# Six steps of attention issued ahead of the branch on the mask, split and reordered input loads, and a later load of expert 1's weights

## The chip, the cores and the metric

One NeuronCore of one Trainium2 chip runs the whole program. The metric is the device time of one execution in microseconds (us), median of several runs. All times below are from one profiled execution unless the text says otherwise; its clock starts at the span's start.

## The reference, cut to what matters

`x` is 2048 x 256, the context 1601 x 256, all float32. The layer is a gated cross attention followed by a gated mixture of experts:

```python
x = x + tanh(g_xattn) * xattn(layernorm(x), ctx, mask)   # 16 heads of 64, Wq, Wk, Wv, Wo
x = x + tanh(g_ffn)   * moe(layernorm(x))                # 8 experts, top 2, hidden 512

scores = einsum('bthd,bThd->bhtT', q, k) / sqrt(64)
scores = where(mask, scores, finfo(float32).min)
attn   = softmax(scores);  out = einsum('bhtT,bThd->bthd', attn, v) @ Wo
# moe: out += (silu(x @ W1[e].T) * (x @ W2[e].T)) @ W3[e].T * w_e  for the two chosen experts
```

The mask of this case lets every query see only the last 401 of the 1601 keys (or fewer). The kernel reads the whole mask, finds out whether that is so, and branches: a fast attention over the last 401 keys, or a general one over all keys. In every run here the fast one is taken.

## The kernel before, in words

The five engines run their own instruction streams and meet at semaphores: PE (TensorE) does the matmuls, ACT (ScalarE) exponentials and most copies out of PSUM, DVE (VectorE) masking, maxima and the block transposes, POOL (GpSimd) the scaling by 1/sum and the scatters, SP (SyncE) only issues DMAs, in program order, all on one queue.

**The opening.** SP issues the loads: the last 401 columns of the context and Wk (both count on `kv_in`), x in four groups of 512 rows (`x_in[g]`), Wq, the mask in four parts of 800 KB (`mask_in[c]`), Wv, Wo, Wg. PE waits for `kv_in`, computes the keys of all eight head pairs (`kT`, L1143), transposes the first 512 normalised rows (`transpose_xn`, L1160) and computes the queries of chunk 0 (L1149). DVE normalises x group 0, takes the statistics of groups 1 to 3, and reduces the last columns of each mask part (L813). ACT copies keys and queries out of PSUM and sums the other mask words (`mask_words`, L605), four passes. POOL turns each mask part into a bias (L462). Then DVE reduces the flag, PE sums it over partitions with a one-column matmul, DVE compares it, and every engine waits for `flag_ready`, reads `plainflag` and branches (`last_block_only`). `settled` makes each engine wait for the rest of the opening, in the fast branch of DVE and POOL too.

**The fast attention** is a hand-written software pipeline of 140 steps (`STEPS_FAST`). A chunk is one head pair for 512 queries (32 chunks); it has four "duos" d (128 queries, two heads), one per step. In step n:

- PE: scores of duo n (`scores`, L1216); in steps 0 to 7 one eighth of V (`values`, L1227), in steps 8 to 10 the late transposes of x; the queries of the next chunk when n % 4 is 1; from step 11 on probabilities times V of an older chunk in two halves (`probs_v`, L1241), from step 18 on half an output projection every fourth step (L1251).
- DVE: in steps 0 to 5 two rows of tiles normalised; the reciprocal of duo n-1's sums, mask and row minimum of duo n (L984), block transposes of duo n-2 (L996).
- ACT: the exponentials of duo n (L636), copies of V, of queries and of attention outputs.
- POOL: scaling of duo n-1 (L525).
- SP and ACT: 16 "regroup" DMAs for each chunk (L316) that move the transposed blocks from `blocksT` across partitions into `probsT`. SP issues 12 of them and ACT 4 (8 each for the last chunk). `probs_v` of a chunk waits for all 16.

Scores of duo d wait until DVE has masked duo d-2 (four PSUM banks); each eighth of V waits until ACT has copied the one before (`v_ready`), since they share one bank.

**The end of attention.** SP loads expert 0's three weight matrices (1.5 MB) in chunk 29, the regroups of chunks 30 and 31, then expert 1's 1.5 MB, then waits for the last regroups, for the schedule of tiles (`sched_ready`) and for the scatters of the regrouped rows (`scattered`), and loads the first tiles of rows (`load_tile`, L353). The expert stage runs 128-row tiles, expert after expert, each with 8 + 8 matmuls and two transposes on PE; routing of the last 512 rows is interleaved with its first tiles. Every tile's result is added to the output by an indirect DMA from POOL.

Of the kernel before, what the change touches and what calls it, by code (L numbers as in the profile page):

```python
# [13 lines left out]
P = 128  # L14
# [51 lines left out]
SCHED_STEP = 133  # L66
LAST_WO = DUOS + 10
# [8 lines left out]
def build(nc, x, ctxT, mask, g_xattn, g_ffn, Wq, Wk, Wv, Wo, WgT, W1T, W2T, W3T, out):  # L76
    with ExitStack() as ctx:
# [64 lines left out]
        with ExitStack() as attn:  # L142
# [3 lines left out]
            with ExitStack() as fast:  # L146
# [4 lines left out]
                with ExitStack() as early:  # L151
                    wk_sb = sb("wk_sb", [P, KT, H * HD], F32, early)
                    mask8 = sb("mask8", [P, NT, SKP], U8, early)
                    xn = sb("xn", [P, GT, D], F32, early)
# [9 lines left out]
                inv_sum = sb("inv_sum", [P, RING_P], F32, fast)  # L164

# [34 lines left out]
        x_in, w_in, g_in = [sem(f"x{g}_in") for g in range(NR)], sem("w_in"), sem("g_in")  # L200
        wo_in = sem("wo_in")
        kv_in, wv_in = sem("kv_in"), sem("wv_in")
# [81 lines left out]
        def settled(eng):  # L284

            eng.wait_ge(w_in, 16)
            eng.wait_ge(wo_in, 16)
            eng.wait_ge(q_ready, 1)
            eng.wait_ge(k_ready, HP)
            eng.wait_ge(wv_in, 16)  # L290
            eng.wait_ge(xnT_ready, 2)
            eng.wait_ge(biases_ready, MASK_DMAS)
            eng.wait_ge(words_seen, MASK_DMAS)
            eng.wait_ge(mask_seen, MASK_DMAS)

# [29 lines left out]
        def _(sp):  # L325
            sp.dma_start(ctx_last[:, :, 0:LASTK], ctxT[:, LAST0:].rearrange("(k p) n -> p k n", p=P)).then_inc(kv_in, 16)
            sp.dma_start(wk_sb[:, :, :], Wk.rearrange("(k p) n -> p k n", p=P)).then_inc(kv_in, 16)
            for g in range(NR):
                sp.dma_start(xs[:, GT * g:GT * g + GT, :], x[g * GQ:(g + 1) * GQ, :].rearrange("(t p) d -> p t d", p=P))\
                  .then_inc(x_in[g], 16)  # L330
            sp.dma_start(wq_sb[:, :, :], Wq.rearrange("(k p) n -> p k n", p=P)).then_inc(w_in, 16)
            sp.wait_ge(mask_pad, 1)
            for c in range(MASK_DMAS):
# [21 lines left out]
            with sp.If(last_block_only(sp)):  # L355
# [81 lines left out]
        def _(pool):  # L437
            pool.memset(mask8[:, :, SKP - 4:], 0).then_inc(mask_pad, 1)
            pool.dma_start(gates[:, 0:1], g_xattn.partition_broadcast(P)).then_inc(g_in, 16)
            pool.dma_start(gates[:, 1:2], g_ffn.partition_broadcast(P)).then_inc(g_in, 16)  # L440
# [19 lines left out]
            for c in range(MASK_DMAS):  # L460
# [55 lines left out]

            def fast_attention():
                settled(pool)

                def scale(d):  # L520

                    pool.wait_ge(inv_ready, d + 1)
                    u = 2 * d % RING_P
                    duo = probs[:, u:u + 2, 0:LASTK]
                    pool.tensor_tensor(duo, duo, inv_sum[:, u:u + 2].unsqueeze(2).to_broadcast([P, 2, LASTK]), ALU.mult)\  # L525
                        .then_inc(scaled, 1)

                for n in range(STEPS_FAST):
                    if n == 2:
                        pool.memset(probsT[:, :, NS - 1, :, :, :], 0.0).then_inc(pads_set, 1)  # L530
                    if 1 <= n <= DUOS:
                        scale(n - 1)
                    r, s = group_of(n)
# [965 lines left out]
```

## Time and profile before

| | us |
|---|---|
| median of 3 runs | 665.11 |
| lowest and highest run | 661.04, 665.76 |
| the profiled execution's own time | 661.78 |
| its span, first to last instruction | 660.0 |
| mean granted clock of PE | 0.986 of full speed |
| PE busy | 622.1 (94%) |
| DVE, ACT, POOL busy | 393.6, 287.7, 309.2 |

The profiled execution has 1.8 us outside its span. A line of a group gives the code line, engine, operation and tiles, then the count, busy time and mean duration in ns, then the idle time before it and who ended it. Matmul durations in a timeline overlap, since matmuls are pipelined, so the distance between two starts is the better price.

### The profile page before, as it was taken

The page shows a single profiled execution, that of the slowest core. Times are in us where ns is not written, and L with a number is a line of the kernel's source. Part 1 is how long each engine was busy: PE and PEld are TensorE (multiplying, and loading weights), DVE is VectorE, ACT ScalarE, POOL GpSimd, SP SyncE. Part 2 cuts the span into 40 slices and gives each one's busy share as a digit, 9 for nine tenths or more (in the row PEclk, how much of TensorE's full clock was granted, in tenths as well). Part 3 has the DMA queues.
Part 4 walks back from the last instruction along what each step waited for, and adds up shares of the span by engine and source line. Part 5 has one row for each costly group of instructions (what it writes and reads, how often), then busy time and mean ns, then how long its engine had stood idle before and what let it go on. Part 6 is the DMA issues. An engine that isn't in the chain of part 4 may idle for free.

```text
span 660.0 us, 10752 instructions
## 1 busy us (share of the span) xinstructions
PE 622.1 (94%) x2958; PEld 346.2 (52%) x2959; DVE 393.6 (60%) x1187; ACT 287.7 (44%) x744; POOL 309.2 (47%) x272
## 2 busy tenths in 40 slices
PE   4599999999999999999999999699999999999994
PEld 2244445454555544455554555256666666666663
DVE  3767788888987878988769977333251212221211
ACT  1556665656555564564545554023322222222221
POOL 2345565555564587564685564502464222222221
PEclk9989999999999999999999998899999999999998
DMA  8904577676766776757677569969556322333221
GB/s 273 333 1 104 144 168 170 142 167 146 163 149 150 161 186 163 166 130 184 134 193 179 135 158 249 269 186 377 161 142 131 49 41 42 47 48 48 46 23 22
DMA packets 92652, 95.37 MB, mean 144 GB/s; under 512 B 11056, under 2 KB 86704, under 8 KB 92592
## 3 DMA queue, kind: packets, MB, share of 16 engines
q1 hardware_dynamic: 69968, 71.64, 41.9%
q10 hardware_dynamic: 15840, 14.07, 9.4%
q0 software_dynamic: 6784, 8.95, 8.2%
q8 instruction: 27, 0.44, 0.3%
q14 instruction: 33, 0.27, 0.1%
HBM read 27.72 MB, written 12.36 MB: 61 GB/s over the span
## 4 chain that ended last, share of the span: by engine, by line
PE 77%; POOL 6%; DMA 5%; issue 4%; DVE 4%; ACT 2%; ACTq 1%; POOLq 0%; SPq 0%; DVEq 0%
PE ps_s L1396 17%; PE ps_s L1216 14%; PE ps_o L1241 13%; PE ps_o L1424 8%; PE ps_a L1149 7%; PE ps_a L1251 7%; POOL probs L525 3%; POOL x_regrouped L513 2%; DMA out_dram<-yg,ids 2%; PE ps_o L1227 2%; PE ps_t L1417 2%; PE ps_s L1143 2%; DVE blocksT L996 2%; DMA probsT<-blocksT 1%; DMA wk_sb<-Wk_dram 1%
## 5 line engine op out<-in xcount | busy, mean ns | idle before, releaser
L525 POOL TENSOR_TENSOR probs<-probs,inv_sum 128x802 f32<-128x802 f32 x128 | 194.8, 1524 | 154.5 <-DVE inv_sum L975 153.7
L636 ACT ACTIVATE probs<-probs,neg_max 128x401 f32<-128x401 f32 x256 | 159.3, 624 | 147.1 <-DVE neg_max L984 147.0
L984 DVE CUSTOM_DVE_ANT_0 probs<-ps_s,biases 128x401 f32<-128x401 f32 x256 | 136.9, 573 | 52.5 <-PE ps_s L1216 51.6
L1396 PE MATMUL ps_s<-w_sb,xgT 128*128 x296 | 139.5, 594 | 1.4 <-ACT xgT L732 1.4
L996 DVE STREAM_TRANSPOSE blocksT<-probs 128x832 f32<-128x832 f32 x128 | 133.2, 1040 | 9.0 <-POOL probs L525 9.0
L564 POOL DMA_INDIRECT out_dram<-yg,ids x36 | 56.0, 1555 | 159.4 <-DVE yg L1108 136.5
L1241 PE MATMUL ps_o<-probsT,v_sb 128*64 128x512 f32 x512 | 125.0, 612 | 4.4 <-DMA probsT<-blocksT 4.4
L1216 PEld LDWEIGHTS ps_s<-kT,qT 64*128 64x128 f32 x1024 | 82.9, 187 | 78.6 <-DVE neg_max L984 42.2
L1216 PE MATMUL ps_s<-kT,qT 64*128 64x201 f32 (+1 forms) x1024 | 122.0, 357 | 1.4 <-issue 1.4
L1096 DVE TENSOR_TENSOR gated<-ps_s,silu 128x512 f32<-128x512 f32 x37 | 25.6, 692 | 117.5 <-PE ps_s L1396 112.1
L1396 PEld LDWEIGHTS ps_s<-w_sb,xgT 128*128 128x128 f32 x296 | 53.0, 191 | 39.5 <-issue 37.9
L745 ACT COPY gatedT<-ps_t 128x512 f32<-128x512 f32 x36 | 21.1, 585 | 120.4 <-PE ps_t L1417 120.4
L1424 PE MATMUL ps_o<-w_sb,gatedT 128*128 x288 | 68.1, 380 | 0.0
L1251 PE MATMUL ps_a<-wo_sb,oT 128*128 128x256 f32 x240 | 61.5, 400 | 3.3 <-ACT qT L593 3.0
L1149 PE MATMUL ps_a<-xnT,wq_sb 128*128 128x512 f32 x128 | 63.2, 616 | 0.8 <-ACT xnT L597 0.8
L1241 PEld LDWEIGHTS ps_o<-probsT,v_sb 128*64 128x64 f32 x512 | 31.7, 137 | 58.9 <-issue 53.4
L1424 PEld LDWEIGHTS ps_o<-w_sb,gatedT 128*128 128x128 f32 x288 | 52.0, 191 | 5.5
L1251 PEld LDWEIGHTS ps_a<-wo_sb,oT 128*128 128x128 f32 x240 | 44.2, 194 | 16.2 <-ACT qT L593 9.6
L636 ACT ACTIVATION_READ_ACCUMULATOR probs<-probs,neg_max 128x1 f32 x256 | 47.8, 187 | 0.0
L1108 DVE TENSOR_SCALAR yg<-ps_o,xg 128x256 f32<-128x256 f32 x36 | 17.4, 484 | 41.3 <-PE ps_o L1424 41.3
L513 POOL DMA_INDIRECT x_regrouped<-rows,place x32 | 31.5, 984 | 9.1 <-issue 8.3
L1149 PEld LDWEIGHTS ps_a<-xnT,wq_sb 128*128 128x128 f32 x128 | 21.9, 189 | 23.9 <-issue 23.9
(142 smaller groups left out, 420.9 us busy)
## 6 DMA issues: line engine op xcount, KB each, us to landing
probsT<-blocksT SPq DMA_DIRECT2D x285, 96.0 KB
probsT<-blocksT SPq DMA_DIRECT2D x95, 128.0 KB
probsT<-blocksT ACTq DMA_DIRECT2D x99, 96.0 KB
xg<-x_regrouped SPq DMA_DIRECT2D x39, 129.0 KB, 2.1
probsT<-blocksT ACTq DMA_DIRECT2D x33, 128.0 KB
w_sb<-W1T_dram SPq DMA_DIRECT2D x8, 512.0 KB, 9.5
w_sb<-W2T_dram SPq DMA_DIRECT2D x8, 512.0 KB, 10.2
w_sb<-W3T_dram SPq DMA_DIRECT2D x8, 512.0 KB, 10.5
```

The costliest lines, as they stand in the source:

```text
L513: pool.indirect_dma_start(out=x_regrouped, out_offset=bass.IndirectOffsetOnAxis(ap=place[:, c, t:t + 1], axis=0), in_=rows[:, c, t, :], in ...
L525: pool.tensor_tensor(duo, duo, inv_sum[:, u:u + 2].unsqueeze(2).to_broadcast([P, 2, LASTK]), ALU.mult)\
L564: pool.indirect_dma_start(out=out, out_offset=bass.IndirectOffsetOnAxis(ap=ids[:, k % RING:k % RING + 1], axis=0), in_=yg[:, k % 2, :], in ...
L636: act.activation(probs[:, b, 0:LASTK], probs[:, b, 0:LASTK], ACT.Exp, bias=neg_max[:, b:b + 1], scale=-1.0, accum_out=sum_exp[:, b:b + 1]) ...
L984: dve.tensor_tensor_reduce(probs[:, b, 0:LASTK], ps_s[u % 4][:, 0:LASTK], biases[:, tile, :], HD ** -0.5, 3e38, ALU.add, ALU.min, neg_max[ ...
L996: dve.transpose(blocksT[:, c % 2, :, :, t * 32:(t + 1) * 32].rearrange("p c u n -> p u c n"), probs[:, u:u + 2, :].rearrange("p u (c n) -> ...
L1149: mm = pe.matmul(ps_a[:, :], wq_sb[:, k, p * P:(p + 1) * P], xnT[:, k, i * GQ:(i + 1) * GQ], start=(k == 0), stop=(k == KT - 1))
L1216: mm = pe.matmul(ps_s[(2 * d + odd) % 4][:, k0:k1], qT[h0:h0 + HD, c % 2, t * P:(t + 1) * P], kT[h0:h0 + HD, c % HP, k0:k1], start=True, s ...
L1241: mm = pe.matmul(ps_o[odd * HD:(odd + 1) * HD, :], v_sb[:, s, 2 * (c % HP) + odd, :], probsT[:, c % 2, s, :, odd, :], start=(s == 0), stop ...
L1251: mm = pe.matmul(wo_bank(g, half)[:, n * D:(n + 1) * D], oT[:, c % 4, t * P:(t + 1) * P], wo_sb[:, c % HP, :], start=(c == 2 * g), stop=(c ...
L1396: mm = pe.matmul(bank[:, :], xgT[:, buf, k, :], w_sb[:, bass.ds(expert, 1), (n * KT + k) * FH:(n * KT + k + 1) * FH].squeeze(1), start=(k ...
L1424: mm = pe.matmul(ps_o[:, 0:D], gatedT[:, k, :], w_sb[:, bass.ds(expert, 1), 2 * KT * FH + k * D:2 * KT * FH + (k + 1) * D].squeeze(1), sta ...
```

## The change

1. **Loads (SP).** The order becomes: x group 0, context, first half of Wk (`kv_in`), first half of Wq (`w_in[0]`), mask part 0, Wv, mask parts 1 to 3, second half of Wk (`wk1_in`), x groups 1 to 3, second half of Wq (`w_in[1]`), the two gates (two tiny DMAs that POOL issued before), Wo, Wg.
2. **Six steps (`PRE = 6`) ahead of the branch.** Steps 0 to 5 of all engines are issued before the flag is read. PE makes keys of pairs 0 and 1 only, then the transposes and queries of chunk 0, then the steps; the other keys come in steps 0, 6, 7, 8, 10 and 12. V moves two steps later (steps 2 to 9), the late transposes of x to steps 20 to 22. The flag's matmul is in step 5. ACT's mask pass c + 1, DVE's and POOL's parts of the mask are in steps 0 to 2 or 3; the tanh of the gates is in step 6.
3. **LayerNorm of x groups 1 to 3 (DVE).** Statistics in steps 6 to 9, three tiles each, the reciprocal square root in step 10, normalising in steps 11 to 16.
4. **`settled`** is waited for only in the general branch. Two tiles get memory of their own (`wk_sb`, `xn`), and the mask pass writes its unused result to `blocksT` instead of `probs`.
5. **Expert 1.** SP issues `load_expert(1)` after the wait for the last regroups instead of before it.

The diff, cut:

```diff
+PRE = 6
+K_STEPS = {0: 2, 6: 3, 7: 4, 8: 5, 10: 6, 12: 7}
+XN_STEP = 20
...
+            load_x(0)
+            sp.dma_start(ctx_last[:, :, 0:LASTK], ...).then_inc(kv_in, 16)
+            load_half(wk_sb, Wk, 0, kv_in)
+            load_half(wq_sb, Wq, 0, w_in[0])
+            sp.wait_ge(mask_pad, 1)
+            load_mask(0)
             sp.dma_start(wv_sb[:, :, :], Wv.rearrange("(k p) n -> p k n", p=P)).then_inc(wv_in, 16)
+            for c in range(1, MASK_DMAS):
+                load_mask(c)
+            load_half(wk_sb, Wk, 1, wk1_in)
+            for g in range(1, NR):
+                load_x(g)
+            load_half(wq_sb, Wq, 1, w_in[1])
...
-                load_expert(sp, 1)
                 expert_there(0)
                 for slot in range(2):
                     sp.wait_ge(probsT_in[slot], 16 * REGROUP * CHUNKS // 2)
+                load_expert(sp, 1)
                 sp.wait_ge(sched_ready, 2)
                 sp.wait_ge(scattered, 16 * 2 * GT * (NR - 1))
...
 # ACT
+            def step_of(n):
+                if n == PRE:
+                    gates_tanh()
+                if 3 <= n < 3 + 2 * NS:
+                    values(n - 3)
+                if n - 1 in K_STEPS:
+                    keys(K_STEPS[n - 1])
...
+                if n < DUOS:
+                    exps(n)
+                if n + 1 < MASK_DMAS:
+                    mask_words(n + 1)
...
+            keys(0)
+            keys(1)
+            move_xnT(0)
+            move_xnT(1)
+            queries(0)
+            mask_words(0)
+            for n in range(PRE):
+                step_of(n)
...
 # DVE
+            def step_of(n):
+                if n == PRE - 1:
+                    flag_everywhere()
+                if PRE <= n < PRE + 4:
+                    statistics(GT + 3 * (n - PRE), GT + 3 * (n - PRE) + 3)
+                if n == PRE + 4:
+                    mean_and_rsqrt(GT, NT, 11)
+                if PRE + 5 <= n < PRE + 11:
+                    for t in (2 * (n - PRE - 5), 2 * (n - PRE - 5) + 1):
+                        normalise(GT + t)
...
+                if n == PRE - 3:
+                    mask_flag()
...
 # PE
+            def step_of(n):
+                if n == PRE - 1:
+                    pe.wait_ge(flag_step, 5)
+                    pe.matmul(ps_t[1][0:1, 0:1], ones[:, 0:1], rowflag[:, 0:1], start=True, stop=True).then_inc(flag_sum, 1)
+                r, s = group_of(n)
+                if n < DUOS:
+                    scores(n)
+                if 2 <= n < 2 + 2 * NS:
+                    values(n - 2)
+                if n in K_STEPS:
+                    if K_STEPS[n] == 4:
+                        pe.wait_ge(wk1_in, 16)
+                    keys(K_STEPS[n])
...
+            keys(0)
+            keys(1)
+            transpose_xn(0)
+            transpose_xn(1)
+            pe.wait_ge(w_in[0], 16)
+            pe.wait_ge(xnT_ready, 2)
+            queries(0)
+            for n in range(PRE):
+                step_of(n)
```

POOL's `step_of(n)` does `mask_biases(n)` for n below 4 and `scale(n - 1)`; its memset of `probsT` moves from step 2 to step 5, behind waits for the three users of the mask tile, whose memory `probsT` shares.

## Rows read from the trace of the kernel before

**Rows 1.** The page: busy time of an engine, and its costliest groups

```profile
PE 622.1 (94%) x2958; PEld 346.2 (52%) x2959; DVE 393.6 (60%) x1187; ACT 287.7 (44%) x744; POOL 309.2 (47%) x272
...
L984 DVE CUSTOM_DVE_ANT_0 probs<-ps_s,biases 128x401 f32<-128x401 f32 x256 | 136.9, 573 | 52.5 <-PE ps_s L1216 51.6
...
L996 DVE STREAM_TRANSPOSE blocksT<-probs 128x832 f32<-128x832 f32 x128 | 133.2, 1040 | 9.0 <-POOL probs L525 9.0
```

**Rows 2.** Busy time of the engines by stretch, with granted clock

```profile
22.40:33.04 10.64, 3.02 (x14) 1.43 (x13) 6.07 (x16) 7.08 (x12) 4.81 (x5) 0.87 0.87 306
33.04:38.00 4.96, 4.96 (x14) 2.62 (x16) 2.64 (x9) 1.44 (x5) 0.93 (x1) 0.60 0.00 0
...
55.14:100.61 45.47, 44.16 (x249) 22.61 (x248) 36.71 (x102) 30.58 (x84) 24.58 (x17) 1.00 0.68 156
```

**Rows 3.** Timeline of the opening: start, length, engine, line, operation

```profile
9.69 12.71 PE L1143 MATMUL ps_s<-ctx_last,wk_sb 128*128 128x401 f32 x32 [9.69 <-DMA wk_sb<-Wk_dram]
...
14.36 0.51 ACT L590 ACTIVATE kT<-ps_s 128x401 f32<-128x401 f32 x1 [1.11 <-PE ps_s L1143]
...
15.70 0.51 ACT L590 ACTIVATE kT<-ps_s 128x401 f32<-128x401 f32 x1 [0.84 <-PE ps_s L1143]
16.20 4.01 DVE L794 BATCH_NORM_STATS2 halves<-xs 128x6 f32<-128x256 f32 x12
...
22.23 1.04 PE L1160 MATMUL ps_t<-ident,xn 128*128 128x128 f32 x8
...
26.08 0.58 ACT L593 COPY qT<-ps_a 128x512 f32<-128x512 f32 x1 [0.94 <-PE ps_a L1149]
...
26.56 1.21 ACT L605 ACTIVATE probs<-mask 128x1200 f32<-128x1200 int32 x1
26.62 1.53 POOL L462 TENSOR_SCALAR biases<-mask 128x1604 bf16<-128x1604 uint8 x1 [0.66 <-DMA mask<-mask_dram]
...
27.95 1.21 ACT L605 ACTIVATE probs<-mask 128x1200 f32<-128x1200 int32 x1
...
33.04 1.71 PE L1216 MATMUL ps_s<-kT,qT 64*128 64x201 f32 x8 [1.38 <-issue]
...
35.37 0.63 ACT L636 ACTIVATE probs<-probs,neg_max 128x401 f32<-128x401 f32 x1 [4.72 <-DVE neg_max L984]
```

**Rows 4.** Timeline of PE alone, steps 4, 5, 6 and 23

```profile
48.72 1.99 PE L1227 MATMUL ps_o<-wv_sb,ctx_last 128*128 128x512 f32 x4
50.63 0.95 PE L1216 MATMUL ps_s<-kT,qT 64*128 64x201 f32 x8
...
55.14 0.95 PE L1216 MATMUL ps_s<-kT,qT 64*128 64x201 f32 x8
...
100.61 0.95 PE L1216 MATMUL ps_s<-kT,qT 64*128 64x201 f32 x8
```

**Rows 5.** The chain that ended last, end of attention

```profile
414.96 9.22 DMA probsT<-blocksT
...
424.22 3.68 PE ps_o L1241 x16
...
432.35 0.40 PE ps_t L1391 x2
```

**Rows 6.** Busy time by stretch, one microsecond of attention's end

```profile
416.00:417.00 1.00, 1.00 (x4) 0.24 (x2) 0.00 (x0) 0.00 (x0) 0.69 (x2) 0.50 1.16 200
```

**Rows 7.** DMA packets, 415.3 to 420.4 and 420.4 to 422.4

```profile
DMA packets 1186, 1.08 MB, mean 211 GB/s; under 512 B 168, under 2 KB 1175, under 8 KB 1186
...
DMA packets 398, 0.64 MB, mean 318 GB/s; under 512 B 66, under 2 KB 254, under 8 KB 398
```

**Rows 8.** Timeline of SP's queue at attention's end

```profile
415.27 0.67 SPq L274 DMA_DIRECT2D w_sb<-W1T_dram  x1
...
416.52 0.57 SPq L274 DMA_DIRECT2D w_sb<-W3T_dram  x1
429.97 8.77 SPq L353 DMA_DIRECT2D xg<-x_regrouped  x8
```

More of the change, by code:

```diff
@@ L198, in build @@
         ps_a = psum("ps_a")
-        x_in, w_in, g_in = [sem(f"x{g}_in") for g in range(NR)], sem("w_in"), sem("g_in")
+        x_in, w_in, g_in = [sem(f"x{g}_in") for g in range(NR)], [sem("w0_in"), sem("w1_in")], sem("g_in")
         wo_in = sem("wo_in")
-        kv_in, wv_in = sem("kv_in"), sem("wv_in")
+        kv_in, wk1_in, wv_in = sem("kv_in"), sem("wk1_in"), sem("wv_in")
         mask_in = [sem(f"mask{c}_in") for c in range(MASK_DMAS)]
@@ L458, in _, with mask_biases @@
                       allow_small_or_imprecise_dtypes=True).then_inc(const_ready, 1)
[L460 removed]
+            def mask_biases(c):
                 pool.wait_ge(mask_in[c], 16)
@@ new lines, in exps, with values @@
+            def exps(d):
+                for u in (2 * d, 2 * d + 1):
+                    b = u % RING_P
+                    act.wait_ge(masked_ready, u + 1)
+                    act.activation(probs[:, b, 0:LASTK], probs[:, b, 0:LASTK], ACT.Exp, bias=neg_max[:, b:b + 1],
+                                   scale=-1.0, accum_out=sum_exp[:, b:b + 1]).then_inc(probs_ready, 1)
+            def values(c):
+                s, half = c // 2, c % 2
+                w = TAIL if s == NS - 1 else P
+                act.wait_ge(pads_ready, 2)
+                act.wait_ge(v_ps, c + 1)
+                act.copy(v_sb[0:w, s, 8 * half:8 * half + 8, :],
+                         ps_o[0:w, :].rearrange("p (h d) -> p h d", h=8)).then_inc(v_ready, 1)
@@ L1036, in _ @@
+            for n in range(PRE):
+                step_of(n)
+            def fast_attention():
+                for n in range(PRE, STEPS_FAST):
+                    step_of(n)
             with dve.If(last_block_only(dve)):
@@ new lines, in scores @@
+            def scores(d):
+                c, t = d // GT, d % GT
+                if t == 0:
+                    pe.wait_ge(q_ready, c + 1)
+                    if c < HP:
+                        pe.wait_ge(k_ready, max(2, c + 1))
+                if d >= 2:
+                    pe.wait_ge(masked_ready, 2 * d - 2)
+                for k0, k1 in ((0, 201), (201, LASTK)):
+                    for odd in range(2):
+                        h0 = odd * HD
+                        mm = pe.matmul(ps_s[(2 * d + odd) % 4][:, k0:k1], qT[h0:h0 + HD, c % 2, t * P:(t + 1) * P],
+                                       kT[h0:h0 + HD, c % HP, k0:k1], start=True, stop=True)
+                        if k0:
+                            mm.then_inc(scores_ready, 1)
@@ new lines, in values @@
+            def values(c):
+                s, half = c // 2, c % 2
+                w = TAIL if s == NS - 1 else P
+                if c == 0:
+                    pe.wait_ge(wv_in, 16)
+                else:
+                    pe.wait_ge(v_ready, c)
+                for k in range(KT):
+                    mm = pe.matmul(ps_o[0:w, :], ctx_last[:, k, s * P:s * P + w],
+                                   wv_sb[:, k, half * 512:(half + 1) * 512], start=(k == 0), stop=(k == KT - 1))
+                mm.then_inc(v_ps, 1)
@@ new lines, in out_projection, with halves_before @@
+            def out_projection(g, half):
+                pe.wait_ge(oT_ready, 2 * g + 2)
+                for n in range(2):
+                    t = 2 * half + n
+                    for c in (2 * g, 2 * g + 1):
+                        mm = pe.matmul(wo_bank(g, half)[:, n * D:(n + 1) * D], oT[:, c % 4, t * P:(t + 1) * P], wo_sb[:, c % HP, :],
+                                       start=(c == 2 * g), stop=(c == 2 * g + 1))
+                mm.then_inc(wo_ps, 1)
+            def halves_before(n):
+                return max(0, min(CHUNKS, (n - 15) // 4))
```

468 lines of the change are left out of this document (213 added, 255 removed).

## The prediction, made before the changed kernel was run

> **What bounds the kernel now.** I read the page first: PE is busy for 94% of the span and no other engine for more than 60% [rows 1]. So the end moves when PE stands still for less, or works at a higher clock, and an edit to DVE or SP counts only where PE waits for it. Next the busy time by stretch, to find where PE does stand still. From the end of the first queries to the first scores it works 3.0 of 10.6 us, and in the 5 us behind that it is busy at a mean granted clock of 0.60. From step 6 to step 23 (55.14 to 100.61) it works 44.16 of 45.47 us [rows 2], so there is nothing to win there, and whatever is won before step 6 stays won. Third, the opening's timeline: scores of step 0 start at 33.04, with everything that they need except the flag there since the query copy at 26.66; the last 1.38 us are the branch ("issue") [rows 3]. Last, the chain at the end of attention: 9.22 us pass from the last regroup's issue to its landing at 424.2, then 8.1 us of PE work for the last chunk, and then the transpose of the first expert tile at 432.35 [rows 5].
>
> **Part 1: when does step 6 start?** I follow the new program with the old durations.
>
> Kv_in: the same 1.46 MB is ahead of it as before (x group 0 and half of Wk in place of the second half), and keys started at 9.69 [rows 3]. But it is now about 1,024 pieces in place of 512 (x rows are 1 KB, half rows of Wk 2 KB, whole ones 4 KB). The trace doesn't price that at the start. From below it is 0, since bytes are equal; from above 2.2 us, 512 pieces more at the 1,186 packets in 5.1 us of the regroups [rows 7]. I take 0.7, nearer the lower end, since the opening's loads read long rows from DRAM. Keys: 10.4.
>
> Two keys, not eight: before, the second was in PSUM at 14.36, that is 4.7 us after the start, cold clock included [rows 3]. So 15.1. Transposes to copied queries took from 22.23 to 26.66, 4.4 us, paced by PE and ACT in turn [rows 3]; xn is ready in time: it was by 16.2 before, when DVE went on to the other groups [rows 3], and x group 0 now lands first. Scores of step 0: 19.5, and not 33.0.
>
> From there ACT is what is late. One mask pass costs 1.4 us (26.56 to 27.95), two exponentials 2 x 0.63 = 1.3, a key copy 0.5, a query or V copy 0.6 [rows 3]. ACT's order is: mask pass 0, exps 0, pass 1, key copy, exps 1, pass 2, query copy, exps 2, pass 3, first V copy. That is 4 x 1.4 + 3 x 1.3 + 0.5 + 0.6 + 0.6 + 0.2 of waiting = 11.4, so V's first eighth is copied at 30.9. The masks are there: before, POOL got the last part at 26.6 [rows 3] after 7.9 MB; now 6.3 MB go ahead of it, so it lands at about 22, and pass 3 starts at 29. PE meanwhile has done steps 1 and 2 and step 3's scores, and stands for about 2 us. From 30.9 it is the bound: three eighths of V at 1.91 (48.72 to 50.63), two scores at 0.9 and one set of queries at 1.9 [rows 4] make 9.4, so step 5 ends at 40.3. The branch costs up to 1.38 [rows 3], or nothing if PE still has matmuls queued while it is taken; the flag is compared some 5 us ahead of it. I take 0.7. **Step 6 starts at 41.0, before at 55.14** [rows 4].
>
> But less has been done by then. Five of the eight keys are still to come, at 1.34 each (14.36 to 15.70) [rows 3] 6.7 us, and two eighths of V more than before, 3.8 us. The stretch to step 23 took 45.47 and becomes 45.47 + 6.7 + 3.8 = 56.0; I take off 0.2 of its 1.31 idle [rows 2], since queued keys cover some of it: 55.8. The late transposes only move inside it. Step 23: 41.0 + 55.8 = 96.8, before 100.61. **Part 1 gains 3.8 us.** The bulk of the 14 us was work postponed, not removed: what really goes is the idle time at 26 to 33 and the half-clock stretch behind it, and 2 us of new idle time, 0.7 of branch and 0.7 of loads come in.
>
> Its ends: with kv_in on time, a covered branch and no idle time in the stretch, 0.7 + 0.7 + 0.9 more, 6.1. With kv_in at the upper end and the branch in full, 2.2 less; with DVE's burst (below) on top, 0 to 0.5.
>
> POOL: it does four mask biases at 1.53 [rows 3] and the scalings beside each other, some 3 us a step in steps 1 to 3, where ACT's steps last 3.3. The bigger memset in step 5 stands in front of scaling 4, wanted by DVE only in step 6. Nothing. SP: the two gate DMAs are now in its queue behind the loads; nobody reads them before step 6. SP's own branch comes at about 37 and its first regroups with it; they are wanted in step 11, some 20 us later. Nothing. PE's wait for `wk1_in` in step 7 is for bytes landed by 25. Nothing.
>
> The LayerNorm of groups 1 to 3 lay in the opening for free. Now it sits in DVE's steps 6 to 16. Statistics cost 4.01 / 12 = 0.33 each [rows 3], 1.0 a step for four steps; step 10 has some 23 small operations, about 3.3 us (estimate: between the statistics' end at 20.2 and the next engine-bound work there was room for no more than 6); then 0.7 a step. A DVE step is 2 x 0.5 + 1.0 + 0.2 = about 2.2 [rows 1]. Over the eleven steps: 24 + 4 + 3.3 + 4.2 = 35.5. PE has 0.9 x 11 scores, four eighths of V, five keys, two queries, four halves of probabilities times V at 1.87: 35.6. A tie, with DVE starting earlier and two steps of slack through the banks. I book 0, with 2 us against.
>
> **Part 2: expert 1 later.** The packets decide it. Between 415.3 and 420.4 all but 11 of 1,186 packets are under 2 KB, so they are regroups, though expert 1's loads are issued from 415.27 on: they lie behind SP's regroups in the same queue [rows 7, 8]. Only between 420.4 and 422.4 are larger ones there, 144 of 398, and many of these belong to POOL's scatter [rows 7]. So expert 1 meets only the last microsecond of ACT's regroups. I take 0.4 us; ends 0 and 2.2, the time that PE stands before 424.22 if a landing is delayed wholly by it.
> The Trainium skill (DMA: Bandwidth & Descriptors, "Queues, rings and completion order") says that each DMA engine takes turns between the queues by packets and keeps order in one. By the first half the edit should free half of the bandwidth for ACT's regroups; by the second it frees nothing until SP's own are through, and the trace agrees with that half.
> The other side: expert 1's 1.5 MB now stand in SP's queue ahead of the row tiles (L353), which were issued from 429.97 [rows 8], just in time for 432.35 [rows 5]. Issued at 424, 1.5 MB take 4.9 us at 318 GB/s and 7.4 at the regroups' 211 [rows 7], and the row tile itself 2.4 from issue to transpose; so that starts at 431.3 or at 433.8. It costs nothing up to about 432, 1.5 at the worst. Expert 1 itself is wanted some tiles later.
>
> **The sum.** 3.8 + 0.4 = 4.2 us less than the profiled 661.78 gives 657.6. That execution stands 3.3 below the median of the three runs, 665.11, which themselves spread over 4.7. Against the median: **660.9**.
>
> **The rivals.**
>
> *A. More than this: the waits go without replacement.* Step 6 at 39.6, and the last regroups land up to 2 us earlier, so that PE's hole before 424.22 closes: 6.1 + 2 = 8 us, 657. For it: PE does stand there for 2.2 us. Against it: the packet sizes [rows 7].
>
> *B. DVE's LayerNorm burst or a cold clock takes most of it.* In step 10 DVE is away for 3.3 us while PE has only 2.2 us of work. And PE idles 2 us in step 3; in attention's end, after two such gaps, it was granted 0.50 for several microseconds [rows 6]. One such spell costs half its length, about 2 us, DVE's jam 0 to 2. Left: 0 to 2 us, 664.
> The Trainium skill (TensorE: Matmul & The Clock Gate, "HAM oscillation") warns that gaps between bursts bring PE back to 1.2 GHz, again and again; it speaks against a kernel that starts attention early but in pieces.
>
> *C. Slower.* The whole head stays at 1.2 GHz. Steps 0 to 5 hold 18 us of PE work (six scores 5.3, four eighths 7.6, a key, two queries) strung between ACT's mask passes. If their gaps keep the granted clock at one half, as in 33 to 38 [rows 2], 18 us more are needed, of which 2 are the idle time: 665.11 + 16 - 4 = 677. It decides from the point where more than 8 us of PE work are done at half clock. Against it: from 19.5 to 28 PE has work nearly without a gap.
>
> *D. No change.* The first row tile behind expert 1 costs 1.5 [rows 5, 8] and kv_in 2.2: what is left is 1 us, 664.
>
> **How the numbers follow.** Forecast 0.50 (its own range 658 to 663), A 0.20, B 0.20, C 0.04, D 0.06. The range needs A's better half, B and D, and the 4.7 by which runs of the same kernel differ: 654.5 to 665.0. The kernel can tell about 1% from no change, 6.6 us. Faster by more needs A, or the forecast's upper end with a favourable median: 0.22. Slower by over 1% is C and a rest: 0.04. Between: 0.74.
>
> **What would show it.** Right: scores of step 0 at 19 to 20, a hole of 1.5 to 2.5 us in PE in step 3 ended by ACT's first V copy, step 6 at 40 to 42, step 23 near 97, the last regroup landing no more than 0.5 us earlier against the first scores of step 127. Wrong: PE waiting for DVE in steps 10 to 13, granted clock under 1 between 13 and 45, kv_in after 11.5, or PE waiting for a row tile at the end of attention. Most of all I may be wrong in ACT's order of copies and passes, since every microsecond there is one of the total.

## The result: 656.6 us, and the profile after

The changed kernel takes 656.64 us (median of 4 runs, 655.02 to 657.84), the kernel before 665.01 on the same chip (661.04 to 665.76). The ratio is 0.988 with a 95% interval of 0.984 to 0.991: faster by 8.4 us, 1.2%. The forecast was 660.9, so the direction was right and the gain half of what came. The profiled execution after took 657.01 us, that of before 661.78; these two are only 4.7 apart, and why that pair shows less than the medians is the first thing to find out. Medians and ratios here and below leave out two executions that stand far apart from all others: one of the kernel before beside experiments 1 to 4 (1264.92 us) and one of experiment 3 (906.37 us).

**Where it went, by marks.** In each trace I note the start of the scores of steps 0, 6, 23 and 127 and of the first expert tile's transposes. This splits the span into a head, a stretch that nothing in the change should touch (23 to 127), attention's end, and the experts.

| start at (us) | step 0 | step 6 | step 23 | step 127 | first tile | span |
|---|---|---|---|---|---|---|
| before | 33.04 | 55.14 | 100.61 | 401.72 | 432.35 | 660.0 |
| after | 18.56 | 38.38 | 94.30 | 395.22 | 427.60 | 655.3 |

The head gains 6.3 at step 23 and 6.5 at step 127; from there to the first tile the new kernel takes 32.4 and the old one 30.6, so 1.7 is given back; from the tile to the end both take 227.7.

The page after, engine PE:

```profile
PE 622.2 (95%) x2958; PEld 344.4 (53%) x2959; DVE 389.9 (59%) x1187; ACT 286.9 (44%) x744; POOL 308.2 (47%) x270
```

PE is as busy as before, 622.2 against 622.1 [rows 1]: no work was removed, only idle time. The windows of the head (columns: stretch, length, then busy time and instructions of PE, weight loads, DVE, ACT, POOL; granted clock, DMA share, GB/s):

```profile
18.56:38.38 19.82, 18.31 (x79) 8.77 (x79) 14.16 (x46) 15.59 (x39) 12.68 (x9) 1.00 0.61 200
38.38:94.30 55.92, 55.02 (x278) 27.48 (x277) 45.76 (x147) 33.59 (x90) 25.94 (x18) 1.00 0.58 133
```

In steps 0 to 5 PE works 18.31 of 19.82 us; before, in the 10.6 us ahead of step 0 alone, it worked 3.0 [rows 2]. Its clock is at the full 2.4 GHz, where before it stood at a mean of 0.60 behind that gap [rows 2]. The timeline of the opening, engines PE and ACT:

```profile
8.57 5.67 PE L1220 MATMUL ps_s<-ctx_last,wk_sb 128*128 128x401 f32 x8 [8.57 <-DMA wk_sb<-Wk_dram]
...
14.27 0.51 ACT L632 ACTIVATE kT<-ps_s 128x401 f32<-128x401 f32 x1 [2.15 <-PE ps_s L1220]
...
18.40 1.21 ACT L648 ACTIVATE blocksT<-mask 128x1200 f32<-128x1200 int32 x1
...
18.56 0.95 PE L1284 MATMUL ps_s<-kT,qT 64*128 64x201 f32 x8 [0.68 <-ACT qT L636]
...
21.52 1.20 ACT L648 ACTIVATE blocksT<-mask 128x1200 f32<-128x1200 int32 x1
...
24.32 1.20 ACT L648 ACTIVATE blocksT<-mask 128x1200 f32<-128x1200 int32 x1
...
25.52 0.57 ACT L636 COPY qT<-ps_a 128x512 f32<-128x512 f32 x1
...
27.22 1.20 ACT L648 ACTIVATE blocksT<-mask 128x1200 f32<-128x1200 int32 x1
...
28.41 0.57 ACT L680 COPY v_sb<-ps_o 128x512 f32<-128x512 f32 x1
...
29.03 1.98 PE L1297 MATMUL ps_o<-wv_sb,ctx_last 128*128 128x512 f32 x4 [1.51 <-ACT v_sb L680]
...
36.56 1.88 PE L1227 MATMUL ps_a<-xnT,wq_sb 128*128 128x512 f32 x4
```
```profile
38.38 0.95 PE L1284 MATMUL ps_s<-kT,qT 64*128 64x201 f32 x8
...
94.30 0.95 PE L1284 MATMUL ps_s<-kT,qT 64*128 64x201 f32 x8
```

Read it against the steps of the prediction: keys at 8.57, second key copied from 14.27, scores of step 0 at 18.56, ACT's four mask passes (18.40, 21.52, 24.32, 27.22) between the copies, V's first copy at 28.41, and PE standing 1.51 us for it. That is the only hole of the six steps. Step 6 starts at 38.38 with no bracket behind it: it comes straight behind the queries of 36.56, so the branch is hidden.

The chain at attention's end, and SP's queue there:

```profile
408.48 9.27 DMA probsT<-blocksT
...
417.79 3.68 PE ps_o L1311 x16
...
425.92 1.69 issue
427.60 0.42 PE ps_t L1486 x2
```
```profile
417.82 0.38 SPq L277 DMA_DIRECT2D w_sb<-W1T_dram  x1
...
418.87 0.47 SPq L277 DMA_DIRECT2D w_sb<-W3T_dram  x1
421.14 8.75 SPq L384 DMA_DIRECT2D xg<-x_regrouped  x8
```

The last regroup takes 9.27 us to land (before 9.22 [rows 5]), though expert 1 is now issued only behind it, at 417.82. So part 2 seems to have won nothing. And PE now stands 1.69 us before the first tile, whose rows are issued at 421.14, behind expert 1's three matrices. That looks like what rival D priced at 1.5, but it isn't a wait for the rows. The time from issue to landing of the eight row tiles (`xg`):

```profile
DMA to landing us min/median/max: 2.2/3.5/4.5
```

Even the slowest of them takes 4.5 us, so the first has landed by 425.6, before the last output projection ends at 425.9. The chain books the 1.69 us as "issue": PE waits for nothing that the profile shows. What part 2 is worth is settled by runs, not by one pair.

### The profile page after: what moved, and what is told of

Same layout as the page of the kernel before. It is cut to its first block, busy times and chain, and to the rows that moved or that the text cites. A ratio compares the mean times of both kernels' runs of the same rounds, so it can differ in the third digit from the quotient of the medians.

```text
span 655.3 us, 10748 instructions
## 1 busy us (share of the span) xinstructions
PE 622.2 (95%) x2958; PEld 344.4 (53%) x2959; DVE 389.9 (59%) x1187; ACT 286.9 (44%) x744; POOL 308.2 (47%) x270
## 4 chain that ended last, share of the span: by engine, by line
PE 76%; POOL 6%; DMA 5%; DVE 5%; issue 4%; ACT 3%; ACTq 1%; SPq 0%; POOLq 0%; DVEq 0%
PE ps_s L1491 17%; PE ps_s L1284 13%; PE ps_o L1311 13%; PE ps_o L1519 8%; PE ps_a L1227 7%; PE ps_a L1321 7%; POOL probs L552 3%; POOL x_regrouped L543 2%; DMA out_dram<-yg,ids 2%; PE ps_t L1512 2%; DVE blocksT L1052 2%; PE ps_o L1297 2%; DVE probs L1040 2%; DMA probsT<-blocksT 1%; PE ps_t L1486 1%
## 5 line engine op out<-in xcount | busy, mean ns | idle before, releaser
L1491 PEld LDWEIGHTS ps_s<-w_sb,xgT 128*128 128x128 f32 x296 | 53.0, 190 | 39.6 <-issue 38.0
L1321 PEld LDWEIGHTS ps_a<-wo_sb,oT 128*128 128x128 f32 x240 | 43.7, 192 | 16.4 <-ACT qT L636 10.1
```

Of the source, the lines that this page charges most:

```text
L1321: mm = pe.matmul(wo_bank(g, half)[:, n * D:(n + 1) * D], oT[:, c % 4, t * P:(t + 1) * P], wo_sb[:, c % HP, :], start=(c == 2 * g), stop=(c ...
L1491: mm = pe.matmul(bank[:, :], xgT[:, buf, k, :], w_sb[:, bass.ds(expert, 1), (n * KT + k) * FH:(n * KT + k + 1) * FH].squeeze(1), start=(k ...
```

## Experiments

The three groups ran on three chips. The kernel before beside them took 664.54 (experiments 1 to 4), 664.63 (5 to 8) and 665.08 us (9 to 12). Ratios are to that, with their 95% interval. The marks of all traces:

| kernel | step 0 | step 6 | step 127 | first tile | 127 to tile | span | median | ratio |
|---|---|---|---|---|---|---|---|---|
| 1 before again | 32.46 | 54.78 | 401.36 | 435.50 | 34.1 | 663.2 | 665.46 | 1.001 |
| 2 expert 1 ahead of the wait | 17.33 | 37.15 | 393.90 | 427.55 | 33.7 | 655.1 | 656.81 | 0.987 |
| 3 expert 1 behind the tiles | 17.78 | 37.59 | 394.44 | 427.96 | 33.5 | 655.6 | 657.38 | 0.987 |
| 4 before, expert 1 late | 31.80 | 53.77 | 400.45 | 433.85 | 33.4 | 661.6 | 665.19 | 1.001 |
| 5 old load order | 20.43 | 42.05 | 398.86 | 431.21 | 32.4 | 658.9 | 661.63 | 0.995 |
| 6 ACT's last mask pass later | 18.23 | 37.44 | 394.20 | 427.26 | 33.1 | 655.0 | 656.72 | 0.987 |
| 7 branch first | 25.07 | 45.09 | 401.93 | 434.76 | 32.8 | 662.3 | 664.58 | 1.000 |
| 8 useless matmuls at the end | 18.45 | 38.26 | 394.99 | 428.25 | 33.3 | 657.6 | 657.66 | 0.988 |
| 9 expert 0 last | 18.48 | 38.29 | 395.09 | 425.60 | 30.5 | 655.0 | 656.06 | 0.986 |
| 10 experiments 6 and 9 | 17.69 | 36.90 | 393.70 | 424.16 | 30.5 | 653.5 | 654.84 | 0.985 |
| 11 before, third trace | 32.11 | 54.28 | 400.88 | 437.64 | 36.8 | 665.3 | 667.20 | 1.003 |
| 12 one mask pass of four on ACT | 17.78 | 36.02 | 392.82 | 426.05 | 33.2 | 653.7 | 655.12 | 0.985 |

**1. The kernel before, unchanged.** Is its spread of 4.7 us two kinds of execution, or scatter?

> The kernel before, unchanged, against itself. Its four runs were 661.0, 664.9, 665.1 and 665.8, a gap of 4 us with nothing in it, and the profiled execution of before (661.8) was one of the low kind. Theory S (two kinds of run): the runs fall again near 661 and near 665, and if the profiled one is of the high kind, its trace shows where the 3.4 us are. Theory N (plain scatter): values spread evenly from 660 to 666. Ratio 1.000 either way.

Measured: 665.46 (12 runs, 661.14 to 670.1), ratio 1.001 (0.998 to 1.004). Together with the 22 runs beside it, these times fill the range without two heaps, so it is scatter. It goes with PE's clock all the same: of 70 runs of this kernel, those with a mean granted clock of 0.985 took 662.9 on average (16 runs), with 0.983 665.6 (24), with 0.981 667.7 (10); the rest have values between and beside. The trace of experiment 1 places it: step 127 at 401.36, 0.4 from the first trace's, but 34.1 us from there to the first tile and not 30.6.

**2. Expert 1 ahead of the wait for the last regroups** (part 2 of the change undone):

```diff
+                load_expert(sp, 1)
                 expert_there(0)
                 for slot in range(2):
                     sp.wait_ge(probsT_in[slot], ...)
-                load_expert(sp, 1)
```

> The changed kernel with expert 1's load back in front of the wait for the last regroups (the change's last part undone). Theory Q (queue order): the first row tile no longer lies behind expert 1's 1.5 MB in SP's queue; PE's 1.69 us without work ahead of the first tile's transposes go, the last regroup lands as before or 0.1 us later: 1.5 us less than the changed kernel (span about 653.8). Theory R (regroups relieved): the later load had made the last regroup land earlier, so undoing it costs 0.5 to 2 us.

Measured: 656.81, ratio 0.987 (0.984 to 0.991), as the changed kernel. The chain at attention's end:

```profile
407.17 10.39 DMA probsT<-blocksT
...
417.60 5.38 PE ps_o L1311 x16
...
427.55 0.43 PE ps_t L1486 x2
```

The hole before the tile is nearly gone (0.13 us). But the regroup lands after 10.39 us in place of 9.27, and the last chunk's work takes 5.38 and not 3.68, partly at half clock, so PE reaches the tile that much later. Nothing is won. Nor does this show that the rows were late in the changed kernel: in both traces they had landed before PE was ready for them. In every trace but those of experiments 9 and 10 that is so, and still PE stands there for up to 2.16 us: 0.72 to 2.16 us in the seven with expert 1 between the wait and the row tiles, 0 to 0.63 in the other five. What it waits for the profile doesn't show. In the program, the end of the fast branch lies at this place, where PE's stream jumps over the general attention; that this is the cause is a guess that no run tests.

**3. Expert 1 behind the first eight row tiles.**

```diff
-                load_expert(sp, 1)
                 sp.wait_ge(sched_ready, 2)
                 ...
                 for k in range(RING):
                     load_tile(0, k)
+                load_expert(sp, 1)
```

> The changed kernel with expert 1's load moved further back, behind the first eight row tiles. Theory Q: the first tile is transposed right after the last output projection, 1.6 us less than the changed kernel (span about 653.7), the same as with the early load or 0.1 better, since the scatter too is undisturbed. Rival: SP issues the tiles for 8.8 us, so expert 1 lands late and PE waits for it at its first tile (the third or fourth, some 17 us after the first): then no gain or a loss.

Measured: 657.38 (5 runs), ratio 0.987 (0.983 to 0.991). The hole is 0.53, the landing 9.87, the last chunk 5.38: the 1.2 us won before the tile aren't in the total.

**4. The kernel before with part 2 alone** (the edit of the change, nothing else).

> The kernel before with only the change's last part: expert 1's load behind the wait for the last regroups. Theory Q: 1.5 us more than before (span 661.5 against 660.0 where both are of the low kind), with a hole of about 1.6 us in PE ahead of the first tile's transposes. Theory R: 0.5 to 2 us less than before.

Measured: 665.19, ratio 1.001 (0.998 to 1.003). Part 2 is worth nothing that 12 runs can see. Its trace has a fast landing, 8.24, and a slow last chunk, 6.67:

```profile
413.71 8.24 DMA probsT<-blocksT
...
421.99 6.67 PE ps_o L1241 x16
...
433.10 0.75 issue
```

**5. The old order of loads in the changed kernel** (whole matrices still in halves, but one behind the other):

```diff
-            load_x(0)
             sp.dma_start(ctx_last ...).then_inc(kv_in, 16)
             load_half(wk_sb, Wk, 0, kv_in)
+            load_half(wk_sb, Wk, 1, wk1_in)
+            for g in range(NR):
+                load_x(g)
             load_half(wq_sb, Wq, 0, w_in[0])
+            load_half(wq_sb, Wq, 1, w_in[1])
             sp.wait_ge(mask_pad, 1)
-            load_mask(0)
+            for c in range(MASK_DMAS):
+                load_mask(c)
             sp.dma_start(wv_sb ...)
-            for c in range(1, MASK_DMAS):
-                load_mask(c)
-            ...
```

> The changed kernel with the loads in the order of before (context, Wk, x, Wq, mask, Wv; the halves stay, each pair side by side). Theory ACT-bound: the head is set by ACT's chain of copies, exponentials and mask passes, which starts with step 0's biases; with mask part 0 landing at 20 as before and Wv only at 29, step 0's masking moves from 19.7 to about 21.7 and V's first eighth from 24.7 to 29.5, so step 6 comes 3 us later (38.4 becomes about 41.5) and the whole 3 us later, 660. Rival (the order is idle dressing, all comes from running ahead of the flag): step 6 within 1 us of 38.4, time as the changed kernel, 657.

Measured: 661.63 (12 runs), ratio 0.995 (0.992 to 0.997). PE in its timeline, and the window behind the gap:

```profile
5.85 5.68 PE L1218 MATMUL ps_s<-ctx_last,wk_sb 128*128 128x401 f32 x8 [5.85 <-DMA wk_sb<-Wk_dram]
...
14.10 1.09 PE L1236 MATMUL ps_t<-ident,xn 128*128 128x128 f32 x8 [2.56 <-DVE xn L860]
...
16.01 3.75 PE L1225 MATMUL ps_a<-xnT,wq_sb 128*128 128x512 f32 x4 [0.82 <-ACT xnT L638]
...
20.43 1.71 PE L1282 MATMUL ps_s<-kT,qT 64*128 64x201 f32 x8 [0.68 <-ACT qT L634]
...
28.84 1.98 PE L1295 MATMUL ps_o<-wv_sb,ctx_last 128*128 128x512 f32 x4
```
```profile
15.10:25.30 10.20, 8.71 (x19) 3.78 (x20) 2.31 (x7) 4.93 (x11) 3.82 (x3) 0.50 1.05 386
```

Keys start 2.7 us earlier, but x comes later: PE waits 2.56 us for the LayerNorm and is then granted half speed for 10 us; the same four query matmuls take 3.75 and not 1.96. Step 6 is at 42.05, 3.7 later than with the new order. Here is the cold clock that rival B feared, made by a gap that the new order closes. The Trainium skill (TensorE: Matmul & The Clock Gate, "HAM oscillation") says that gaps between bursts bring PE back to 1.2 GHz; this trace agrees, while the changed kernel, whose gaps there are 0.82, 0.68 and 1.51 us, kept 2.4 GHz. A late landing of Wv, which I had expected to set the pace, isn't waited for: the first eighth of V starts at 28.84, straight behind the scores.

**6. ACT's last mask pass one step later**, so that V's first copy stands ahead of it:

```diff
-                if n + 1 < MASK_DMAS:
-                    mask_words(n + 1)
+                if n in (0, 1, 3):
+                    mask_words({0: 1, 1: 2, 3: 3}[n])
```

> The changed kernel with ACT's last mask pass one step later, behind step 3's V copy and exponentials instead of in front of them. Theory ACT-bound: the V copy at 28.4 comes 1.2 us earlier, PE's hole of 1.5 us ahead of the second eighth of V shrinks to 0.3, and step 6 starts 1.2 us earlier; step 4's V copy may give back up to that much, so 0 to 1.2 us less in all, most likely 0.8. Rival (the pass only moves the hole): step 4's copy is late by the same 1.2, step 6 unchanged at 38.4.

```profile
27.51 1.98 PE L1297 MATMUL ps_o<-wv_sb,ctx_last 128*128 128x512 f32 x4 [0.32 <-ACT v_sb L680]
...
30.89 1.98 PE L1297 MATMUL ps_o<-wv_sb,ctx_last 128*128 128x512 f32 x4 [0.51 <-ACT v_sb L680]
```

Steps 0 to 5 take 19.21 in place of 19.82: the hole of 1.51 becomes 0.32, and the pass makes a new one of 0.51 a step later. The median, 656.72, ratio 0.987 (0.983 to 0.990), can't tell 0.6 us.

**7. Branch first.** All passes over the mask, the flag and the branch stand ahead of step 0 again; the new load order, the late keys and the late LayerNorm stay.

```diff
 # ACT; the other engines alike
-            mask_words(0)
-            for n in range(PRE):
-                step_of(n)
+            for c in range(MASK_DMAS):
+                mask_words(c)
 ...
             def fast_attention():
-                for n in range(PRE, STEPS_FAST):
+                for n in range(0, STEPS_FAST):
                     step_of(n)
```

> The changed kernel with the flag and the branch ahead of step 0 again: all four mask passes, the flag, the branch, then steps 0 to 139; the new load order, the postponed keys and the postponed LayerNorm stay. Theory (running ahead carries the gain): mask part 3 lands at about 21, ACT's passes end at 24, scores of step 0 start near 26 with the clock at one half for some microseconds, step 6 at about 43 to 44 and the whole 5 us slower than the changed kernel, 662. Rival (the load order and the postponed keys carry it): no more than 2 us slower, 659.

```profile
23.53 0.19 PE L1367 MATMUL ps_t<-rowflag,ones 128*1 128x1 f32 x2 [6.84 <-DVE rowflag L873]
...
25.07 1.71 PE L1266 MATMUL ps_s<-kT,qT 64*128 64x201 f32 x8 [1.35 <-issue]
```
```profile
19.00:29.00 10.00, 4.12 (x14) 2.46 (x14) 2.61 (x13) 4.84 (x10) 2.63 (x2) 0.50 1.09 360
```

Measured: 664.58 (12 runs), ratio 1.000 (0.998 to 1.002); step 127 at 401.93, as before. PE stands from the queries to the flag (6.84 us), then 1.35 until it is through the branch (DVE's comparison of the flag, 0.15, then reading it and branching), and does the next steps at half speed. So the load order with the postponed keys and LayerNorm is worth nothing by itself: it brings the first scores from 32 forward to 25, but the postponed keys and V work fall due again. The gain needs work that PE can do while the flag is on its way.

**8. Useless matmuls in PE's holes at attention's end** (five, on a tile of ones and a part of V, with results that nobody reads), to keep its clock up:

```diff
+                if n in (DUOS + 3, DUOS + 7):
+                    for _ in range(3 if n == DUOS + 3 else 2):
+                        pe.matmul(ps_t[0], ones, v_sb[...], start=True, stop=True)
```

> The changed kernel with five matmuls without use (512 columns, result never read) on PE: three ahead of its wait for chunk 30's regroups, two ahead of its wait for chunk 31's. They add work and take none away. Theory (the end's spread is PE's clock): the granted clock stays at full speed through the last two chunks' probabilities times V, 3.7 us each and not up to 5.4 or 6.7, runs spread less and the median falls by 1 to 3 us. Rival (the landings set the end): chunk 31's start does not move, and a warm clock saves only what its own matmuls took more, 0 to 1.7 us, or the five matmuls cost 0 to 1 us.

Measured: 657.66, ratio 0.988 (0.985 to 0.991).

```profile
408.26 9.66 DMA probsT<-blocksT
...
417.96 3.68 PE ps_o L1311 x16
...
426.08 2.16 issue
428.25 0.42 PE ps_t L1489 x2
```

```profile
430.00:434.00 4.00, 4.00 (x7) 1.57 (x6) 0.00 (x0) 0.96 (x2) 0.00 (x0) 0.57 0.91 298
```

The last chunk starts at 417.96, when the regroup has landed, and not sooner (417.79 without): the landing sets that start. Its work runs at full clock, but PE then stands 2.16 us before the tile, and a half-clock stretch follows inside the first tiles (0.57 on average from 430 to 434), where the changed kernel has none: from the tile to the end it takes 229.4 and not 227.7. So the useless matmuls moved the half-clock stretch and didn't remove it.

What PE's clock is worth in this end differs between the kernels. From the start of the last chunk to the tile the kernel before takes 8.1 us with a last chunk of 3.68, and 10.5, 11.9 and 11.3 with 5.38, 6.67 and 6.55 (traces before, 1, 4, 11): there the slow clock is paid in full. In the changed kernel and its variants (9 and 10 apart) it is 8.8 to 10.4, with 9.8 in the changed kernel (3.68) and 9.95 and 10.35 in experiments 2 and 3 (5.38): there the hole before the tile takes up most of the difference.

**9. Expert 0 behind the last regroups** too, and expert 1 behind the row tiles, as in experiment 3. Expert 0's 1.5 MB were issued by SP from 391.17 on, in the middle of the last chunks.

```diff
-                    if c == CHUNKS - 3:
-                        sp.wait_ge(q_ready, CHUNKS)
-                        load_expert(sp, 0)
-                expert_there(0)
...
+                sp.wait_ge(q_ready, CHUNKS)
+                load_expert(sp, 0)
                 for slot in range(2): ...
-                load_expert(sp, 1)
                 ...
-                for k in range(RING): load_tile(0, k)
+                for k in range(2): load_tile(0, k)
+                expert_there(0)
+                for k in range(2, RING): load_tile(0, k)
+                load_expert(sp, 1)
```

> The changed kernel with expert 0's load moved from in front of chunk 30's regroups to behind chunk 31's, and expert 1's behind the first eight row tiles. Theory (the end is set by what lies in SP's queue ahead of the last regroups): the 1.5 MB of expert 0, some 4 us of transfer, no longer stand ahead of both chunks' regroups; chunk 31's land about 3 to 4 us earlier, and if expert 0 is there in time for the first tile the whole is 2 to 4 us less, 653 to 655. Rival (PE's own chain or the scatter sets the end): landings come earlier, but PE then waits for the first row tile, since POOL's eight scatters are issued until 417 whatever is done; 0 to 1 us less. Worse: expert 0 lands behind the first tile, 1 to 3 us more.

```profile
416.49 5.13 DMA x_regrouped<-rows,place
...
422.50 2.96 DMA xg<-x_regrouped
...
425.60 0.42 PE ps_t L1486 x2
```
```profile
427.00:430.00 3.00, 3.00 (x4) 1.04 (x4) 0.00 (x0) 0.71 (x1) 0.00 (x0) 0.50 0.48 122
```

Measured: 656.06, ratio 0.986 (0.982 to 0.989). The last chunk's work starts at 414.22, 3.6 us earlier (in experiment 10, with the same edit, at 412.83), so expert 0 was what the regroups waited behind. But the chain has another member now: GpSimd's scatter of the last routed rows lands at 421.6, only then are row tiles issued (422.50), and PE waits 3.25 us for the first. It comes 2.0 earlier than in the changed kernel; the half-clock stretch right behind it (0.50) makes the rest take 229.4 and not 227.7, and 0.3 of span is left.

**10. Experiments 6 and 9 together.**

> The kernel of the run before this one with ACT's last mask pass one step later. The head gave 0.6 us when this was done alone (step 6 19.2 us after the first scores, not 19.8); here the same 0.6 less than that run.

Measured: 654.84 (653.23 to 656.69), ratio 0.985 (0.982 to 0.988), the fastest kernel of the study, 1.5% under the kernel before. Against the changed kernel it is 1.8 us, too near to be claimed alone; each half shows in the marks (step 6 at 36.90, 30.5 us from step 127 to the tile).

**11. The kernel before, a third trace.**

> The kernel before once more, for another trace. The runs' medians differ by 8 us between before and the change, the heads of the traces only by 6.6 at step 127. Theory L (the first trace of before had a lucky end): its 30.6 us from the scores of step 127 to the first tile's transposes were short, all others lie at 32.4 to 34.1; this trace again has 33 to 34.5, and the difference of the ends between before and the change is 0 to 1 us. Rival: the opening of before varies by more than the 1.3 us seen, through a longer stretch at half clock, and this trace shows step 127 at 403 or later.

```profile
414.13 12.18 DMA probsT<-blocksT
...
426.35 6.55 PE ps_o L1241 x16
...
437.64 0.42 PE ps_t L1391 x2
```

Step 127 is at 400.88, within 0.8 of the other two traces of this kernel, and from there to the tile it takes 36.8 us: the landing 12.18 and the last chunk 6.55 at half clock, where the trace that the prediction worked from had 9.22 and 3.68 [rows 5]. So the scatter between the four traces of the kernel before arises in attention's end, from the landing and from PE's clock, and that first trace had a lucky one.

**12. ACT does one pass over the mask in place of four.** The other three are left out, so that the first 1,200 columns are looked at for a quarter of the rows only.

> The changed kernel without ACT's mask passes 1 to 3: the first 1200 columns of the mask's rows are looked at for a quarter of the rows only; the last 404 columns are looked at for all rows as before. ACT has 4 us less to do ahead of V's first copy. Theory ACT-bound: the hole of 1.5 us in step 3 goes, step 6 starts 18.3 us after the first scores and not 19.8, the whole is 1.5 us less. Rival (something else would be next, PE's wait for masking or V's landing): less than 0.8.

```profile
17.78:36.02 18.24, 18.24 (x79) 8.77 (x79) 13.95 (x46) 12.54 (x33) 13.07 (x10) 1.00 0.72 237
```

Steps 0 to 5 take 18.24 us, and PE is busy in all of them: 1.6 less than with the passes (19.82), and exactly PE's own work. Median 655.12, ratio 0.985 (0.982 to 0.988). ACT's passes cost 1.6 us of the path, and more isn't to be had before step 6.

## Why the prediction came out half the size

**The account.** The kernel before has four traces with its head (before, 1, 4, 11): step 127 on average at 401.1, the spans at 662.5. The changed head with the changed end or one of the two orders of expert 1 has three (after, 2, 3): 394.5 and 655.3. So the head is worth 6.6 us; the end from step 127 to the tile is 33.7 against 33.2 on average, 0.5; together 7.1, of the 7.2 between the spans. The medians say 8.4, with an interval of 5.7 to 10.4 that holds 7.2. Most of the last microsecond is which executions were traced: the four traced ones of the old head took 664.3 on average, 0.8 below the median of those 70 runs of the kernel before (665.1), the three of the new one 657.1. The pair of the first two traces showed only 4.7 because the end of the old one was the shortest of four.

**The step that failed is the size of part 1**, booked at 3.8 and measured at 6.6. By its terms, against the trace after (step 6 at 41.0 forecast, 38.38 measured, 2.6 less):

- *Loads of the first keys:* 10.4 forecast, 8.57 measured. I added 0.7 for more and smaller pieces. They cost nothing that shows: the keys start between 7.8 and 8.8 in the nine traces with the new order. The base was off too: 9.69 [rows 3] was the latest of four; the other three traces with the old kernel have 8.74, 8.76 and 8.69. So 1.1 of this pair's 1.8 is the scatter of one landing.
- *Keys to first scores:* 9.1 forecast, 10.0 measured, 0.9 worse. Before, the second key's copy started 4.7 us after the first matmul, now 5.7, since the slow start of PE lasted longer (last section). In the other traces with this head the stretch takes 9.0 to 10.1, so 9.1 was within its scatter.
- *ACT's chain to V's first copy:* right in kind, PE waits there for ACT's copy as forecast, 1.51 us against "about 2"; but it was booked at 11.4 and took 10.5. I priced a pass by the distance between two passes in a row (26.56 to 27.95 [rows 3], 1.4). Here another instruction follows each pass, and it starts after 1.2 (27.22 to 28.41): four times 0.2 is most of the 0.9.
- *From there to step 6:* 9.4 of work forecast, 9.35 measured; the branch, booked at 0.7, cost 0. Its lower end was the right one: PE still had the queries of 36.56 to do and shows no hole before step 6. In experiment 7, where PE stands waiting for the flag, the flag's comparison, its reading and the branch cost 1.35.

By the sum of these terms the forecast of step 6 was 2.6 too late; the mechanism, work ahead of the flag with ACT as the bound in step 3, was right. The lower end of part 1 was also added up wrongly: 3.8 - 2.2 - 2 is -0.4, not 0 to 0.5.

**What was right.** The stretch from step 6 to 23 was forecast at 55.8 and took 55.92, in experiment 7 too, whose head is another: five keys and two eighths of V postponed are paid in full, and DVE's LayerNorm burst costs nothing. Part 2, booked at 0.4 with 0 as its lower end, is 0 within 0.3% (experiment 4). Of the signs, the hole in step 3 came (1.51 us, ended by ACT's first V copy); step 0, step 6 and step 23 all came earlier than I had said.

**The rivals.** A gave 657, the time that came, with two mechanisms. Its first, loads on time and a covered branch, was right, and stronger than it said (38.4, not 39.6). Its second, the closing hole in the end, didn't happen, so that its figure fits is in part luck. B's DVE jam didn't occur; its cold clock neither, but experiments 5 and 7 show it one change away. C is refuted: 2.4 GHz from 38 to 94, and 1.00 in steps 0 to 5. D priced two landings, and neither is there: the keys came early, and the row tile had landed before PE was ready, by 425.6 against 425.9. PE's hole of 1.69 at that place has another end, which stays open. The chance for faster by over 1% stood at 0.22, since I had put 0.50 on a head whose every unknown was taken near its middle; the landing, the branch and DVE's burst all turned out at their cheap ends.

**What runs show of the cause.** With the six steps behind the branch the whole gain is gone (664.58). With them ahead but the old load order, 3.0 us of it are left (661.63). With both, 8. The order is worth 4.1 us at step 127 (398.86 against 394.7, the mean of the five traces with the changed head), and only as part of running ahead.

## To carry to other kernels

Work that an engine can do without a flag belongs ahead of the flag, not because that removes work (most of it is only postponed) but because it fills the wait, hides the branch and keeps PE from the half-clock stretch that follows a gap; the loads must then be ordered for the new first consumer, or a new gap opens. Take the baseline of a sum from several traces: here one trace put a landing 1 us late and the end of a phase 3 us short. Where a phase ends with a landing behind a full DMA backlog, look at what is issued ahead of it (expert 0: 3.6 us), not at what is issued behind it (expert 1: nothing). And before a hole is put down to the load that stands nearest, look up when that load landed.

## What the runs showed of the hardware

- Regroups within SBUF move at about half the rate of loads at the same full DMA share:

```profile
403.50:413.00 9.50, 6.59 (x17) 2.45 (x17) 2.92 (x14) 0.00 (x0) 6.29 (x14) 0.50 1.15 204
```

  These are 204 GB/s at a share of 1.15, nearly all regroups until the scatter joins in, while the loads of the opening reach 386 at 1.05 (experiment 5, above). So the last regroup lands 8.2 to 12.2 us after its issue in these kernels.
- The same row shows PE granted 0.50 for 9.5 us at full backlog, 6.6 of them busy. A spell of this kind fell somewhere in the end of every trace, at places that differ, and it decides whether the last chunk takes 3.7, 5.4 or 6.6 us. In the traces of experiments 8, 9 and 10, where PE stood 2.16, 3.25 and 3.20 us before the first tile, another followed inside the first tiles; after 1.69, 1.72 and 1.73 us (after, 5, 12) none did.
- The first matmuls of the program run at half speed for a while that differs between traces. PE's weight loads in the kernel before (one line is one or more loads):

```profile
12.49 0.34 PEld L1143 LDWEIGHTS ps_s<-ctx_last,wk_sb 128*128 128x128 f32 x1 [0.33 <-issue]
...
13.14 8.61 PEld L1143 LDWEIGHTS ps_s<-ctx_last,wk_sb 128*128 128x128 f32 x26 [0.32 <-issue]
```

  Until 13.1 they stand 0.67 us apart, from then on 0.33. In the changed kernel all eight matmuls of the first two keys are 0.67 apart (8.57 to 14.04), in experiment 3 only the first five. So the first eight take 4.7 to 5.7 us. The views print a clock of 1.00 for that stretch, but they print it as well for 0 to 5 us, where PE does nothing, so here it isn't evidence; the durations fit the lower of the two levels.
